# Attention's outputs stay in SBUF with their norms taken there; the first local layer's Q and K operands load during attention

## The chip, the cores and the metric

The kernel runs on one NeuronCore of a Trainium2 chip. The metric is the device time of one execution in microseconds (us), taken over several runs; lower is better. One execution is also recorded by the hardware profiler. Engines are called as the profile calls them: PE (TensorE), DVE (VectorE), ACT (ScalarE), POOL (GpSimd) and SP (SyncE, which here only issues DMAs).

## The reference

The input x is 2048 tokens of 128 features. First comes a global attention with 16 heads of 8 features over all 2048 tokens, with a bias made of relations between tokens; then six local layers, each an attention over windows of 32 tokens (16 heads of 64) and a gated feed-forward.

```
def _layernorm(x, axis=-1, eps=1e-05):
    ...
    return (x - m) / jnp.sqrt(v + eps)

x = L0_attn_hidden_states
x = x + attn(_layernorm(x), ...)        # global attention
x = x + ffn(_layernorm(x), ...)         # six local layers, see below

def ffn(x, ...):
    for i in range(DEPTH):              # DEPTH = 6
        x = attn_layer(shift_tokens(x), Wqkv[i], q_scale[i], k_scale[i], Wo[i]) + x
        x = ffn_layer(shift_tokens(x), ln_g[i], ln_b[i], W1[i], b1[i], W2[i], b2[i]) + x
    return x
```

What matters here is the line between the two: the local layers start from the layer norm of the attention's output x1 = x + attn(...), and x1 itself is added once more at the very end.

## The kernel before, in words

All work goes in blocks of P = 128 tokens, NB = 16 of them. Each engine has its own instruction stream, written out without loops at run time, and the streams meet in semaphores. A `nc.Block()` is a section that all engines enter and leave together.

**Global attention.** The function `attention` is one such section. A block of queries has two units (eight heads each), a unit has 16 steps (one for each block of keys), so there are 512 steps. In each step PE makes two score tiles of 128x1024, called a and b: each from the products `queries_keys` (L529) and the bias `relations` (L537). The a tile runs 24 steps ahead and serves only to find the maximum: DVE takes it into `colmax` (`a_max`, L824, or L820 for the first key block of a unit). The b tile goes through Exp on ACT (L660), and PE multiplies it with the values (`values`, L571). The tiles rotate through three PSUM slots. PE's b products of one step go into the slot of the a tile of the step before, so they wait until DVE has read that one. Beside this, DVE, POOL and ACT make the relation probabilities of blocks to come (`largest`, `recip` L837, `scaled` L758 and others), and SP moves them out to DRAM and back (`quarter_out` L989, `quarter_in` L1002), waiting for POOL each time; SP also loads the next queries (L979).

At fixed steps a unit has small events which PE puts through one PSUM bank, `psM`, and which DVE reads in `read_m`. For every second unit these are, among others, "heads" at step 4 and "proj" at step 6; "max0" (four transposes of `colmax`, L586) comes at step 8. DVE reads "proj" in step 7 (L897): it adds the residual `x_res` and writes `x1_sb`, which SP stores to the DRAM tensor `x1` (`store`, L1031). DVE waits for the former store before it writes `x1_sb` again. After the last block SP waits until all of `x1` has landed (L392 in the profile's waits), and the section ends.

**Between attention and the local layers** there is a second section (L1167 to L1203). SP loads all of `x1` back into `xm`, then the rotary tables `rope` (2 MB), `mask32` and `ident` (L1172), then the 22 loads of the first layer's weights (`load`, L1164). POOL fills six tiles with constants (L1179). DVE waits for the four first loads, takes mean and variance of the 16 blocks (L1192, L1196), POOL raises the variances to the power -0.5 (L1184, L1186), and DVE writes the normed `xa` in two instructions over all blocks (L1200, L1203).

**Local layers.** The third section is a software pipeline of 96 units (six layers of 16 blocks), one step for each unit, with seven steps between a unit's first and last operation. In a step PE transposes the block's input (L1341), ACT copies it shifted by one token to `xsT` (L1433 to L1436), PE projects Q, K and V (L1232), DVE rotates Q and K (L1522 to L1524) with tables that POOL makes (`tab`, L1470), POOL adds and scales, SP copies V's windows (L1664), and so on. PE and POOL wait for all 22 loads of a layer (`w_dma`) before its first unit.

## Time and profile before

| | |
|---|---|
| median of 3 runs | 3207.76 us (3205.29 to 3214.18) |
| the profiled execution, its own time | 3208.75 us |
| its span in the profile | 3206.9 us |
| PE busy | 2957.1 us (92%) |
| DVE busy | 2435.7 us (76%) |
| ACT busy | 2083.1 us (65%) |
| POOL busy | 1978.7 us (62%) |

The span runs from the first to the last instruction that the profile shows; the time has 1.85 us more. A share of busy time is a mean over very different stages, so the stages have to be read one by one: preparation and attention up to 1460.7 us, the section between, and the local layers from 1487.5 us to the end. In the timeline's rows the columns are start, duration, engine, line, operation, output and inputs with their sizes, count, and in square brackets the idle time of the engine before it with what ended it. PEclk is the clock that the chip granted to PE, as a share of 2.4 GHz.

### The profile page before, as it was taken

How to read it: one execution, taken by the hardware profiler on the slowest of the kernel's cores; microseconds unless marked ns; L12 is line 12 of the kernel's file. 1: busy time of each engine (PE TensorE's matmuls, PEld its weight loads, DVE VectorE, ACT ScalarE, POOL GpSimd, SP SyncE). 2: the span in 40 equal slices, each digit the busy share in tenths (PEclk: the TensorE clock that was granted, in tenths of full speed). 3: DMA queues.
4: the chain of work that ended last, by engine and by line, in shares of the span. 5: the costliest groups of instructions: out<-in, count | busy, mean ns of one | idle time of the engine just before them, and what ended most of it. 6: DMA issues, size and time to landing. Idle time of an engine off the chain costs nothing. (4 is left out here: it accounts for less than half of the span.)

```text
span 3206.9 us, 122755 instructions
## 1 busy us (share of the span) xinstructions
PE 2957.1 (92%) x53271; PEld 2271.7 (71%) x53271; DVE 2435.7 (76%) x3493; ACT 2083.1 (65%) x2874; POOL 1978.7 (62%) x1720
## 2 busy tenths in 40 slices
PE   4389999999999999994899999999999999999997
PEld 3267777777777777772677777777777777777776
DVE  4777777777787777743788888887887888888884
ACT  2345555555555555543777877877778787787785
POOL 1635555545554554404777777877777777787783
PEclk8599999999999999997999999999999999999998
DMA  4544454445445444403322233223223322422221
GB/s 119 102 80 85 79 87 83 85 79 86 85 86 86 86 85 85 85 5 107 93 67 71 60 91 82 62 71 96 68 69 83 83 62 68 103 61 72 73 71 43
DMA packets 253992, 251.90 MB, mean 79 GB/s; under 512 B 81999, under 2 KB 198624, under 8 KB 253328
## 3 DMA queue, kind: packets, MB, share of 16 engines
q1 hardware_dynamic: 251776, 243.67, 36.3%
q8 instruction: 421, 6.90, 1.0%
q14 instruction: 115, 0.94, 0.1%
q10 hardware_dynamic: 1680, 0.40, 0.1%
HBM read 96.22 MB, written 40.37 MB: 43 GB/s over the span
## 5 line engine op out<-in xcount | busy, mean ns | idle before, releaser
L660 ACT ACTIVATE prob<-psS 128x1024 f32<-128x1024 f32 x512 | 524.1, 1024 | 588.2 <-PE psS L537 580.6
L824 DVE TENSOR_TENSOR colmax<-psS,colmax 128x1024 f32<-128x1024 f32 x480 | 587.2, 1223 | 298.7 <-PE psS L537 297.5
L537 PE MATMUL psS<-diag,pst 128*128 128x64 bf16 x16384 | 584.6, 194 | 21.7 <-issue 21.7
L537 PEld LDWEIGHTS psS<-diag,pst 128*128 128x128 f16 x16384 | 518.1, 99 | 81.9 <-issue 28.2
L1232 PE MATMUL R<-wqkv,xsT 128*128 128x512 f32 x1152 | 551.9, 602 | 20.2 <-DVE gT L1627 8.7
L529 PE MATMUL psS<-qst,kst 48*128 48x128 bf16 (+1 forms) x8192 | 380.7, 220 | 121.5 <-DMA pst<-p_parts 86.0
L758 POOL TENSOR_TENSOR rel<-rel,rec 128x1024 f32<-128x1024 f32 x64 | 151.8, 2372 | 484.1 <-DVE rec L837 484.1
L529 PEld LDWEIGHTS psS<-qst,kst 48*128 48x128 bf16 (+1 forms) x8192 | 235.3, 95 | 277.6 <-issue 166.9
L1358 ACT ACTIVATE kT<-R 64x1024 f32<-64x1024 f32 x192 | 195.5, 1018 | 255.7 <-PE R L1239 254.6
L1454 POOL TENSOR_TENSOR pr<-pr,mx 128x1024 f32<-128x1024 f32 x96 | 182.6, 1902 | 258.3 <-DVE mx L1539 258.3
L571 PE MATMUL psO<-prob,v 128*9 128x128 f32 x8192 | 326.2, 275 | 11.0 <-issue 9.8
L1232 PEld LDWEIGHTS R<-wqkv,xsT 128*128 128x128 f32 x1152 | 198.0, 192 | 167.3 <-issue 151.9
L837 DVE RECIPROCAL rec<-tot 128x128 f32<-128x128 f32 x256 | 238.7, 939 | 0.0
L1463 POOL TENSOR_TENSOR q<-q 128x1024 f32<-128x1024 f32 x96 | 227.3, 2368 | 9.9 <-DVE q L1524 9.9
L1475 POOL TENSOR_TENSOR k<-k 128x1024 f32<-128x1024 f32 x96 | 227.9, 2374 | 0.0
L1283 PEld LDWEIGHTS psA<-wo,otT 128*128 128x128 f32 x1536 | 186.4, 192 | 44.0 <-issue 44.0
L571 PEld LDWEIGHTS psO<-prob,v 128*9 128x9 f32 x8192 | 173.9, 90 | 42.2 <-issue 13.8
L1252 PE MATMUL R<-kT,qT 128*32 128x128 f32 x6144 | 188.5, 275 | 2.2 <-ACT qT L1346 2.2
L1448 POOL TENSOR_TENSOR kn<-k,rn 128x1024 f32<-128x1024 f32 x96 | 182.6, 1902 | 12.7
L1331 PE MATMUL R<-v,prT 128*32 128x128 f32 x6144 | 187.6, 274 | 2.8 <-ACT prT L1346 2.8
L1458 POOL TENSOR_TENSOR pr<-pr,rn 128x1024 f32<-128x1024 f32 x96 | 182.7, 1903 | 7.5
L1283 PE MATMUL psA<-wo,otT 128*128 128x128 f32 x1536 | 187.0, 275 | 0.0
(191 smaller groups left out, 5896.2 us busy)
## 6 DMA issues: line engine op xcount, KB each, us to landing
v<-vs SPq DMA_DIRECT2D x576, 128.0 KB, 2.4
pst<-p_parts SPq DMA_DIRECT2D x512, 128.0 KB, 4.9
p_parts<-stage SPq DMA_DIRECT2D x64, 512.0 KB, 3.0
v<-vs SPq DMA_DIRECT2D x384, 64.0 KB, 2.1
wqkv<-in_L_ffn_Wqkv SPq DMA_DIRECT2D x18, 512.0 KB
q_stack<-qpart SPq DMA_DIRECT2D x6, 512.0 KB
qst<-q_stack SPq DMA_DIRECT2D x32, 96.0 KB, 5.5
wo<-in_L_ffn_Wo SPq DMA_DIRECT2D x6, 512.0 KB
```

What stands on the lines that cost most here:

```text
L529: pe.matmul(dst[:, hp, P * p:P * (p + 1)], kst[r, pair, P * jb:P * (jb + 1)], qst[r, par, pair, :], start=(p == 0), stop=False, skip_group ...
L537: last = pe.matmul(o, pst[:, par, g, P * jb:P * (jb + 1)], diag[:, par, g, h0:h0 + HH // 2, :], start=False, stop=(g == NG - 1), skip_grou ...
L571: last = pe.matmul(psO[32 * c:32 * c + HD + 1, P * s:P * (s + 1)], v9[:, jb, HH * half + hl, :], prob[:, jb % 2, col:col + P], start=(jb = ...
L660: act.activation(prob[:, st % 2, :], psS[:, slot_of("b", st)].rearrange("p a b -> p (a b)"), ACT.Exp)\
L824: dve.tensor_tensor(dst, src, dst, ALU.max).then_inc(a_read, 1)
L837: dve.reciprocal(rec[:, r, cols], tot[:, r, cols]).then_inc(rr_done, 1)
L1232: last = pe.matmul(R[slot[kind, n]][:, c, :], xsT[:, n % 3, :], w[:, INNER * which + 512 * c:INNER * which + 512 * (c + 1)], start=True, s ...
L1252: last = pe.matmul(o[WIN * w:WIN * (w + 1), P * i:P * (i + 1)], qT[:, par, i, WIN * w:WIN * (w + 1)], kT[:, par, i, :, WIN * w:WIN * (w + 2)],
L1283: last = pe.matmul(psA[:, 0:D], otT[:, i, :], wo[:, n // NB % 2, D * i:D * (i + 1)], start=(i == 0), stop=(i == PAIRS - 1))
L1358: act.activation(kT[r, par, :, hp, WIN:WIN + P], keys[r], ACT.Copy)
L1463: pool.tensor_tensor(q1[:, n % 2, :], q1[:, n % 2, :], q2[:], ALU.add).then_inc(m["q_added"], 1)
L1475: pool.tensor_tensor(k1[:], k1[:], k2[:], ALU.add).then_inc(m["k_added"], 1)
```

## The change

1. Attention adds the projection to `x_res` in place; `x_res` now is the part of `xm` from which the local layers read. SP stores each block to DRAM straight from there, since it is still needed at the end. The wait for the former store goes.
2. For blocks 0 to 14 DVE takes mean and variance right behind that addition (`bn_stats`, `bn_aggr`), and POOL makes the root in `root(blk)`, in windows 1 and 5 of each round of attention.
3. Before the last round of attention SP issues nine loads (`local_first`): the first layer's Q and K weights (512 KB each), the rotary tables of blocks 0 and 1, and six rows of scales.
4. The middle section is gone. The former wait for `x1` to land moves to the first use on DVE (unit 0's L1557) and on SP.
5. In the local section each engine starts with its share: SP issues the other 14 loads of layer 0 (V's weights first), ACT issues `mask32` and the other 14 blocks of `rope`, DVE zeroes `xsT`, `zeros`, `xm`'s first row and `kT`, POOL zeroes a half of `vs` and `v2` behind the first `tab`.
6. `xa` is written block by block (`normed`, one `tensor_scalar`): blocks 0 and 1 at the start, block s + 2 at the start of DVE's step s. Block 15 gets its mean, variance and root there too.
7. Waits for weights are split (`weights_here`): for layer 0 there is one for the early loads, one for V, and one for the rest.

```
@@ attention, DVE, "proj"
-                    if not (isinstance(blk, int) and blk == 0):
-                        dve.wait_ge(x1_dma, blk * 16)
-                    dve.tensor_tensor(x1[:], psM[:, 0:D], xr, ALU.add).then_inc(m_read, 1)
+                    dve.tensor_tensor(x_res[:, blk, :], psM[:, 0:D], x_res[:, blk, :], ALU.add).then_inc(m_read, 1)
+                    if blk < NB - 1:
+                        dve.wait_ge(m_read, n + 1)
+                        if blk > 0:
+                            dve.wait_ge(ln_done, blk)
+                        dve.bn_stats(bn1[:], x_res[:, blk, :]).then_inc(ln_st, 1)
+                        dve.wait_ge(ln_st, blk + 1)
+                        dve.bn_aggr(mv16[:, blk, :], bn1[:]).then_inc(ln_done, 1)
@@ attention, POOL
+            def root(blk):
+                pool.wait_ge(ln_done, blk + 1)
+                pool.tensor_scalar(mv16[:, blk, 1:2], mv16[:, blk, 1:2], 1e-5, None, ALU.add).then_inc(ln_root, 1)
+                pool.wait_ge(ln_root, 2 * blk + 2)
+                pool.tensor_tensor(rs16[:, blk:blk + 1], mv16[:, blk, 1:2], minus_half[:], ALU.pow).then_inc(ln_root, 1)
...
+                    if k % 4 == 1 and not (first and k == 1):
+                        root(it * 2 + k // 4 - 1)
@@ attention, SP
+            def local_first():
+                sp.dma_start(shared["wq0"][:], io["Wqkv"][0, :, 0:INNER]).then_inc(shared["first_dma"], 16)
+                sp.dma_start(shared["wk0"][:], io["Wqkv"][0, :, INNER:2 * INNER]).then_inc(shared["first_dma"], 16)
+                sp.dma_start(shared["rope01"][:], io["rope"][:, 0:2, :]).then_inc(shared["first_dma"], 16)
+                ... six rows of scales ...
...
-                sp.dma_start(dst, x1[:]).then_inc(x1_dma, 16)
+                sp.dma_start(dst[:, blk, :], x_res[:, blk, :]).then_inc(x1_dma, 16)
...
             for it in range(1, 7):
                 body(it)
+            local_first()
             body(7, last=True)
             store(NB - 1, 20 * 7 + 20 - 3 + 3)
-            sp.wait_ge(x1_dma, 16 * NB)
@@ local_layers: the section with L1167 to L1203 is removed whole
@@ local_layers, PE
-                        if n % NB == 0:
-                            pe.wait_ge(m["w_dma"], (n // NB + 1) * (16 * NWL))
+                        weights_here(pe, n, 0)
...
+                        else:
+                            pe.wait_ge(m["xa_ready"], n + 1)
@@ local_layers, ACT
+                act.dma_start(mask32[:], io["mask"]).then_inc(m["mask_dma"], 16)
+                act.dma_start(rope[:], io["rope"][:, 2:NB, :]).then_inc(rope_dma, 16)
                 for s in STEPS:
@@ local_layers, POOL, behind the first tab
+                        if n == 0:
+                            pool.memset(vs[:, 1, :], 0.0).then_inc(m["zero_v"], 1)
+                            pool.memset(v2[:], 0.0).then_inc(m["zero_v"], 1)
@@ local_layers, DVE
+                def normed(b):
+                    dve.tensor_scalar(xa[:, b, :], xm[:, b + 1, :], mv16[:, b, 0:1], rs16[:, b:b + 1], ALU.subtract, ALU.mult)\
+                       .then_inc(m["xa_ready"], 1)
+                dve.memset(xsT[:], 0.0).then_inc(m["zero_kT"], 1)
+                dve.memset(zeros[:], 0.0).then_inc(m["zero_kT"], 1)
+                normed(0)
+                normed(1)
+                dve.memset(xm[:, 0, :], 0.0)
+                dve.memset(kT[:], 0.0).then_inc(m["zero_kT"], 1)
                 for s in STEPS:
+                    n = s + 2
+                    if s >= 0 and n < NB:
+                        if n == NB - 1:
+                            dve.wait_ge(m["ln15"], 5)
+                        normed(n)
...
+                        if n == 0:
+                            dve.wait_ge(x1_dma, 16 * NB)
@@ local_layers, SP
             def _(sp):
+                load(sp, 0)
...
+                        if n == 0:
+                            sp.wait_ge(m["zero_v"], 2)
```

## Rows read from the trace of the kernel before

**Rows 1.** Windows: duration, then busy us (instructions) of each engine, PEclk, DMA, GB/s

```profile
1640.00:3190.00 1550.00, 1527.55 (x18454) 1176.79 (x18453) 1248.21 (x1950) 1215.27 (x1852) 1190.55 (x1243) 1.00 0.30 73
```

**Rows 2.** Timeline from attention's last output to the first unit of the local layers

```profile
1460.40 0.29 DVE L897 TENSOR_TENSOR x_sb<-psM,x_res 128x128 f32<-128x128 f32 x1 [0.58 <-PE psM L597]
1460.79 0.34 SPq L1031 DMA_DIRECT2D x<-x_sb  x1
1462.78 0.11 POOL L1179 MEMSET half<- 128x16 f32 x1 [112.44 <-POOLq L392]
...
1463.67 2.03 SPq L1172 DMA_DIRECT2D rope<-in_rope  x1
1464.57 6.92 POOL L1179 MEMSET v<- 128x8192 f32 x1
...
1474.79 3.19 DVE L1192 BATCH_NORM_STATS2 bn<-xm 128x6 f32<-128x128 f32 x16 [14.10 <-DMA ident<-in_ident]
...
1484.93 2.29 DVE L1203 TENSOR_TENSOR xa<-xa,rs 128x2048 f32<-128x2048 f32 x1
...
1487.53 0.45 PE L1341 MATMUL psA<-ident,xa 128*128 128x128 f32 x1 [27.16 <-PEq L1167]
1488.01 0.27 ACT L1433 ACTIVATE xsT<-psA 64x128 f32<-64x128 f32 x1 [31.14 <-PE psA L1341]
...
1488.68 6.93 PE L1232 MATMUL R<-wqkv,xsT 128*128 128x512 f32 x12 [0.70 <-ACT xsT L1436]
...
1492.22 1.22 DVE L1522 TENSOR_TENSOR q<-R,tab 128x1024 f32<-128x1024 f32 x1 [4.99 <-PE R L1232]
...
1494.72 2.36 POOL L1463 TENSOR_TENSOR q<-q 128x1024 f32<-128x1024 f32 x1 [6.48 <-DVE q L1524]
```

**Rows 3.** Groups by line and shape: count, busy us, mean ns, idle before

```profile
L207 DVE MEMSET v<- 128x256 f32 x1 | 0.3, 272 | 0.2 <-issue 0.2
L1604 DVE TENSOR_SCALAR xn<-xs_f,mv,rstd 128x128 f32<-128x128 f32 x96 | 32.4, 338 | 2.0 <-POOL rstd L1487 2.0
L1588 DVE BATCH_NORM_STATS2 bn<-xs_f 128x6 f32<-128x128 f32 x96 | 27.4, 285 | 23.5 <-DMA xs_f<-xm 23.5
L1592 DVE BATCH_NORM_AGGREGATE mv<-bn 128x2 f32<-128x6 f32 x96 | 17.5, 182 | 3.3
L1487 POOL TENSOR_TENSOR rstd<-var,half 128x1 f32<-128x1 f32 x96 | 54.9, 572 | 8.0
```

**Rows 4.** Timeline of attention around one block's L897, DVE and PE

```profile
771.01 0.28 DVE L897 TENSOR_TENSOR x_sb<-psM,x_res 128x128 f32<-128x128 f32 x1
771.21 0.94 DVE L837 RECIPROCAL rec<-tot 128x128 f32<-128x128 f32 x1
...
772.16 1.23 DVE L820 COPY colmax<-psS 128x1024 f32<-128x1024 f32 x1
...
773.66 0.62 PE L529 MATMUL psS<-qst,kst 48*128 48x128 bf16 x16
...
774.89 1.23 DVE L824 TENSOR_TENSOR colmax<-psS,colmax 128x1024 f32<-128x1024 f32 x1 [0.65 <-PE psS L537]
```

**Rows 5.** Timeline of attention: two places where PE stood still

```profile
661.03 0.40 PE L529 MATMUL psS<-qst,kst 51*128 51x128 bf16 x8 [0.44 <-DVE colmax L824]
661.36 1.11 PE L537 MATMUL psS<-diag,pst 128*128 128x64 bf16 x32
...
692.33 0.34 PE L529 MATMUL psS<-qst,kst 51*128 51x128 bf16 x5 [1.54 <-issue]
692.60 1.54 PE L537 MATMUL psS<-diag,pst 128*128 128x64 bf16 x32
```

**Rows 6.** Timeline of SP where attention's last round begins

```profile
1320.82 1.20 SPq L979 DMA_DIRECT2D qst<-q_stack  x2
1331.32 0.38 SPq L989 DMA_DIRECT2D p_parts<-stage  x1
...
1340.61 0.35 SPq L1031 DMA_DIRECT2D x<-x_sb  x1
```

More of the change, by code:

```diff
@@ L386, with attention @@
 WEIGHTS = 9
-def attention(nc, io, keep):
+def attention(nc, io, keep, shared):
     with ExitStack() as ctx:
@@ L431, in attention @@
         guard_dma = sem("guard_dma")
[L432 removed]
+        ln_st = sem("ln_st")
+        ln_done = sem("ln_done")
+        ln_root = sem("ln_root")
         own_done = sem("own_done")
@@ L1054, in global_attention, with local_layers @@
     prepare(nc, io, keep)
-    attention(nc, io, keep)
-def local_layers(nc, io):
+    attention(nc, io, keep, shared)
+def local_layers(nc, io, shared):
     with ExitStack() as ctx:
@@ L1164, in load @@
                     sp.dma_start(dst, src).then_inc(m["w_dma"], 16)
-        with nc.Block() as block:
-            @block.sync
-            def _(sp):
-                for dst, src in ((xm[:, 1:NB + 1, :], io["x1"].rearrange("(b p) d -> p b d", p=P)),
-                                 (rope[:], io["rope"]), (mask32[:], io["mask"]), (ident[:], io["ident"])):
-                    sp.dma_start(dst, src).then_inc(m["init_dma"], 16)
-                load(sp, 0)
-            @block.gpsimd
-            def _(pool):
-                n = 0
-                for tile, value in ((half1[:], -0.5), (vs[:], 0.0), (v2[:], 0.0), (kT[:], 0.0), (zeros[:], 0.0), (xsT[:], 0.0)):
-                    pool.memset(tile, value).then_inc(m["init_pool"], 1)
-                    n += 1
-                pool.wait_ge(m["init_dve"], 2)
-                pool.wait_ge(m["init_pool"], n)
-                pool.tensor_scalar(mv16[:, :, 1], mv16[:, :, 1], 1e-5, None, ALU.add).then_inc(m["init_pool"], 1)
-                pool.wait_ge(m["init_pool"], n + 1)
-                pool.tensor_tensor(rs16[:], mv16[:, :, 1], half1[:, 0:NB], ALU.pow).then_inc(m["init_pool"], 1)
-            @block.vector
-            def _(dve):
-                dve.wait_ge(m["init_dma"], 16 * 4)
-                for b in range(NB):
-                    last = dve.bn_stats(bn16[:, b, :], xm[:, b + 1, :])
-                last.then_inc(m["init_dve"], 1)
-                dve.wait_ge(m["init_dve"], 1)
-                for b in range(NB):
-                    last = dve.bn_aggr(mv16[:, b, :], bn16[:, b, :])
-                last.then_inc(m["init_dve"], 1)
-                dve.memset(xm[:, 0, :], 0.0)
-                dve.wait_ge(m["init_pool"], 8)
-                dve.tensor_tensor(xa[:], xm[:, 1:NB + 1, :], mv16[:, :, 0:1].broadcast_to([P, NB, D]),
-                                  ALU.subtract).then_inc(m["init_dve"], 1)
-                dve.wait_ge(m["init_dve"], 3)
-                dve.tensor_tensor(xa[:], xa[:], rs16[:].unsqueeze(2).broadcast_to([P, NB, D]), ALU.mult)
@@ L1208, in local_layers, with weights_here @@
+        def weights_here(eng, n, part):
+            l = n // NB
+            if n % NB == 0:
+                if l:
+                    eng.wait_ge(m["w_dma"], l * (16 * NWL))
+                elif part == 2:
+                    eng.wait_ge(v0_dma, 16)
+                elif part == 3:
+                    eng.wait_ge(w0_dma, 16 * (NWL - 9))
+                else:
+                    eng.wait_ge(first_dma, 16 * 9)
         RING = (("S", 2), ("Q", 0), ("kT", 1), ("K", 0), ("V", 0), ("qT", 1), ("pT", 2), ("oT", 3), ("h", 5), ("O", 2))
@@ L1440, in _ @@
             def _(pool):
+                pool.memset(half1[:], -0.5).then_inc(m["ln15"], 1)
                 for s in STEPS:
```

119 lines of the change are left out of this document (78 added, 41 removed).

## The prediction

> **What bounds the kernel now.** I read the windows by stage first, to see where PE is the limit. In the local layers it is: PE is busy for 1527.55 of 1550 us at full clock, against 1248.21 us on DVE and 1190.55 us on POOL [rows 1]. So work taken off DVE or POOL there brings nothing, and work put on them costs nothing as long as PE isn't kept waiting. Attention also runs at PE's pace, but its margin is small: DVE stands only fractions of a microsecond between its instructions [rows 4].
>
> Then I read the timeline over the seam, since the change is mostly there. Attention's last output starts on DVE at 1460.40 us, and the first projection of the local layers starts at 1488.68 us [rows 2]. What fills these 28.28 us can be followed in the rows: the store of the last block (1460.79), its landing and the common exit (first instruction of the next section at 1462.78), the four loads until 1474.79, the norms, the end of the section, a transpose at 1487.53, ACT's copies from 1488.01. It is one chain with nothing beside it on PE, so it lies on the path whole. That is the most that the change can take away here.
>
> Last I read the timeline of one block's projection step in attention, because the change puts new DVE work there, 15 times, and the timeline of SP where the new loads go.
>
> **The seam afterwards.** The section of its own is gone, the round trip of x1 through DRAM too. What is left, step by step:
>
> The exit. SP's last act in attention is to issue the store, 1460.79 + 0.34 = 1461.13. Before, the store had to land first, and the next section began 1.65 later, at 1462.78. Where nothing had to land, at the other section's end, the step was short: DVE's last instruction ended at 1484.93 + 2.29 = 1487.22 and PE began at 1487.53, 0.31 later [rows 2]. I take 1461.13 + 0.37 = 1461.5 for the entry into the local section (bounds 1461.2 and, if nothing of the landing is saved, 1462.8).
>
> DVE's share: `xsT` (384 columns), `zeros`, `normed(0)`. The memset of 256 columns took 0.272 us [rows 3], near 1 ns a column, so `xsT` takes about 0.4; `zeros` 0.1 to 0.2; `normed` is the form of L1604, 0.338 [rows 3]. The first `xa` is ready at 1461.5 + 0.9 = 1462.4, and PE's transpose, 0.48 from its start to ACT's [rows 2], ends near 1463.0.
>
> ACT's share: it issues two DMAs before it may copy. The nearest rows are SP's: 2.03 for all 16 blocks of `rope` [rows 2], so 14/16 x 2.03 = 1.78, and 0.34 for a 64 KB store such as `mask32`. ACT comes free at 1461.5 + 2.1 = 1463.6, and with small gaps at 1463.8. That is later than the transpose, so ACT's issuing ends last at the entry. If an issue on ACT takes twice as long as on SP it is 1465.9.
>
> From ACT's first copy to the projection 1488.68 - 1488.01 = 0.67 [rows 2]. The first projection then starts at 1463.8 + 0.67 = 1464.5 (bounds 1463.7 and 1466.6), in place of 1488.68. **The seam gives 24.2 us**, between 22.1 and 25.0.
>
> What could be late next is checked in turn. The Q weights, the K weights, the scales and the first tables came during attention. DVE must have zeroed `kT` before it rotates Q: 5120 columns at near 0.85 ns (POOL's memset of 8192 took 6.92 us [rows 2]; DVE's own rate by its 256 columns is at most 1.06 ns) are 4.4 to 5.4 us, begun at about 1462.9 behind `normed(1)` and the small memset: free at 1467.3 to 1468.3. The rotation needs the projection, which came 1492.22 - 1488.68 = 3.54 us after its start [rows 2], so at 1468.0. The two meet, at most 0.3 is lost; and if PE still ran at full clock after its short rest, DVE would keep it from gaining more than some 0.7. POOL: 0.11 for `half`, some 0.6 for the first table (a quarter of the 2.36 of L1463's 1024 columns), 0.87 for half of `vs` and 6.92 for `v2` [rows 2], 8.5 in all, so it ends at 1470.0; its first addition came 2.50 behind the start of the rotation [rows 2], so it is wanted at 1470.5. Hidden, by half a microsecond. V's weights are the first of SP's loads, beside 1.8 MB of `rope`. The old four loads, 3.1 MB, were there 1474.79 - 1462.78 = 12.0 us after their section's start [rows 2]; 2.4 MB at that pace are 9.3 us, so 1470.8 at worst. V's projection stands third, some 5 us behind Q's, at 1469.6, and ACT takes its result only 5 us later still. Hidden.
>
> The Trainium skill, "Trainium Kernel Development and Optimization", Key Constraints, says of such splits that DMAs issued from SP, ACT and POOL run on the same 16 DMA engines, and that several issuers save issue time alone. That speaks against moving `rope` to ACT's queue, since it would compete with V's weights; no row of before has two such queues at once. By the rule the sum stays as it is, because the bound above lets both share one rate.
>
> **Attention with the norms in it.** Behind L897 DVE now has `bn_stats` (0.285) and `bn_aggr` (0.182) [rows 3], each behind a wait for the one before, which ends the overlap: today the reciprocal starts 0.20 behind the addition [rows 4], afterwards about 0.31 + 0.31 + 0.09 = 0.71 behind. DVE is 0.51 late in 15 blocks. Who waits: the maximum of the next step (L820) would start at 772.67 and end at 773.90 in the block shown. PE's a products of the following step start at 773.66 [rows 4], because the four transposes of "max0" stand before them in this very step; its b products, which need that maximum read, follow 0.28 later at 773.94. So the margin is 0.04 us less the semaphore: PE waits 0.02 to 0.1. The next maximum has 0.65 of idle time before it [rows 4], so the lateness ends there. I take 0.03 a block, 0.5 us in all. Without the transposes' cover it would be the whole 0.51, so 15 x 0.51 = 7.7 us; that is the upper bound. Below zero it can't go: the store's wait that is removed never showed as idle time before L897.
>
> POOL's root is the pair that L1487 belongs to, 0.572 [rows 3] plus a quarter for the addition, some 0.9 us a block. What hides it is POOL's idle time: it is busy for 62% of the span, and in attention its next work in line, `scaled`, waits for DVE's last reciprocal of the window, which comes steps later. Nothing, then; were POOL the limit, it would be 13 us. The place of `root` comes after DVE's `bn_aggr` in time, so nothing queues behind its wait.
>
> SP issues nine more DMAs before the queries at 1320.82 [rows 6]. At 0.34 [rows 2] to 0.60 each (the two at 1320.82 took 1.20) they take 3 to 5.5 us. SP's next appointment is at 1331.32, and the queries are wanted when the a tiles enter the last block, one step behind the projection stored at 1340.61 [rows 6]. Free up to some 10 us; above that it would cost the excess. Their 1.4 MB run where the DMA queues were mostly empty. I take 0.
>
> **The local layers.** `normed` adds 0.338 x 14 = 4.7 us to DVE, and `xa` in bulk (two instructions) has gone from the seam. PE is the limit from the sixth step on, so at most the steps before that can feel it; there DVE mostly stands before its first instruction of a step. I take 0.3, with 0 and 2 as bounds.
>
> **Sum.** 3208.75 (span 3206.9 and the 1.85 around it) - 24.2 + 0.5 + 0.3 = 3185.35 for an execution like the one profiled. Its time lay 1 us above the median of the runs, so by the median 3207.76 - 23.4 = 3184.4. I predict 3185.
>
> **Rivals.**
> The norms stall PE (rival A). DVE's margin of 0.04 is nothing, and two self-waits more than I count would use it up. For it: PE stood 0.44 us where DVE was late by a similar chain [rows 5]. Against: there no transposes lay between. At the bound, 7.7 us come back: 3192.
>
> The entry is slower than I count (rival B): ACT's issues take twice SP's, the landing of the store counts after all, or the first instructions of the section come late; 2 to 5 us come back, 3187 to 3190. For it: no row shows ACT issuing a large load.
>
> It ends slower (rival C): PE's clock. After a stand of 1.54 us PE's next group took 1.54 us where the same group takes 1.11 behind a stand of 0.44 [rows 5], so a stand of that length costs its own time, 0.43 in this group and, as an estimate from it, up to twice that again in the two groups that follow. If the norm's waits kept PE for 1.5 us in each of 15 blocks, this would be 15 x (1.5 + 1.3) = 42 us: 3226. It decides from 24 / 15 = 1.6 us a block, stand and clock together. Against it: my count is a fiftieth of that, and DVE's own part in full is 0.51.
>
> It hardly moves (rival D): DVE's `tensor_scalar` shuts POOL out. The Trainium skill, "SBUF — State Buffer", Who interferes with whom, says that such an instruction in a two-port mode holds the port that POOL reads through. As a mechanism here: POOL would be held 14 times 0.338, 4.7 us, and the memset of `v2` delayed beside it by 1; even together with A that leaves about 10 us of gain, 3198. The row speaks against the mode: 0.338 for 128 columns is no faster than an addition.
>
> **Chances.** My case 0.72, A 0.10, B 0.08, D 0.02, C 0.04, and 0.04 that several of them together eat all but 9 us. This kernel's runs tell about 0.3% (9.6 us) from no change. Faster takes my case, A, B and D, 0.92; same is the 0.04 of the sum of several; slower is C. The range goes from 3180 (the seam at its best, the clock kept) to 3192 (A in full).
>
> **What the profile will show.** The first L1232-like matmul 4 us behind the last output, not 28; ACT's DMA issues last before its first copy; an idle of under 0.1 on PE before the b products one step after the projection; the same distance from transpose to transpose in the local layers. I am wrong if attention ends more than 2 us later than 1460.7, if DVE's memset of `kT` or V's weights end a wait of PE, or if local steps grow.

## The result and the profile after

| | before | after |
|---|---|---|
| median | 3207.76 us | 3226.15 us (3221.13 to 3227.9, 5 runs) |
| ratio | | 1.0045, 95% interval 1.0031 to 1.0060 |
| span of the profiled execution | 3206.9 us | 3224.8 us |
| attention's first and last output | 281.4, 1460.4 us | 283.3, 1487.7 us |
| first projection of the local layers | 1488.68 us | 1498.69 us |
| unit 0's and unit 6's transposes | 1487.53, 1582.39 us | 1497.51, 1595.05 us |

The changed kernel is slower, by 18 us by the medians and by 10 to 19 us by the interval of the ratio, where 23 us of gain were predicted. The window over the local layers, which answers to [rows 1] (duration, busy us of PE, PE's weight loads, DVE, ACT and POOL, then PEclk, DMA share, GB/s):

```profile
1640.00:3190.00 1550.00, 1528.58 (x18502) 1176.04 (x18501) 1253.50 (x1955) 1215.86 (x1855) 1199.93 (x1251) 1.00 0.29 74
```

PE is as busy there as before (1527.55 us in [rows 1]). So most of the loss is elsewhere. The timeline over the seam, which answers to [rows 2]:

```profile
1487.69 0.29 DVE L907 TENSOR_TENSOR xm<-psM,xm 128x128 f32<-128x128 f32 x1 [0.89 <-PE psM L601]
...
1488.83 0.35 ACTq L1350 DMA_DIRECT2D mask<-in_mask  x1
1488.90 0.73 POOL L1480 TENSOR_TENSOR tab<-rope,scale_rows 128x256 f32<-128x256 f32 x1
...
1489.22 0.45 ACTq L1351 DMA_DIRECT2D rope<-in_rope  x1
1489.28 8.18 DVE L1550 TENSOR_SCALAR xa<-xm,mv,rs 128x128 f32<-128x128 f32 x1
...
1489.56 0.95 POOL L1484 MEMSET vs<- 128x1024 f32 x1
...
1490.45 6.93 POOL L1485 MEMSET v<- 128x8192 f32 x1
...
1497.51 0.47 PE L1343 MATMUL psA<-ident,xa 128*128 128x128 f32 x1 [9.86 <-DVE xa L1550]
...
1498.68 4.33 DVE L1558 MEMSET kT<- 128x5120 f32 x1 [1.01 <-issue]
...
1498.69 3.78 PE L1230 MATMUL R<-wq,xsT 128*128 128x512 f32 x4 [0.70 <-ACT xsT L1444]
```

Two things are to be seen. The last output starts 27.3 us later than in [rows 2], at 1487.69 instead of 1460.40. And the first projection stands 11.00 us behind it, not 28.28 as before and not the predicted 4.1: `normed(0)`, an instruction of a third of a microsecond, lasts 8.18 us on DVE and ends just when POOL's three instructions beside it end (1490.45 + 6.93 = 1497.38).

The span's +17.9 us is then made up like this: attention +27.3, the seam -17.3 (28.28 to 11.00), the steps from unit 0 to unit 6 +2.7 (94.86 to 97.54), the later steps +4.2 (below), and about 1 at the end.

Of the +27.3, 1.9 us lie ahead of the first output, and the first output comes at 276 to 285 us in the kernels below, with no order that an edit would explain. The other 25.4 are in attention between its first and its last output, and not in the work that the change put there. In the waits of PE between the first and the last output (what, who ended it: us in total, times, longest), before and after:

```profile
PE psS L537 <- issue: 21.2, 23, 1.6
PE psS L529 <- DVE colmax L824: 14.5, 36, 0.4
PE psO L571 <- issue: 8.7, 12, 1.4
PE psS L529 <- issue: 8.1, 9, 1.5
```

```profile
PE psS L541 <- issue: 32.7, 27, 2.6
PE psS L533 <- DVE colmax L838: 14.1, 35, 0.4
PE psO L575 <- issue: 11.7, 11, 1.9
PE psS L533 <- issue: 11.5, 9, 1.8
```

The waits for DVE's `colmax` are the same, 14.5 and 14.1 us: PE doesn't wait for the norms. What grew is "issue", time in which PE waits for nothing that the profile shows: 38.0 us before (21.2 + 8.7 + 8.1), 57.2 after (the three rows and 1.3 in a fourth). The windows between first and last output show the rest of it:

```profile
281.40:1460.40 1179.00, 1121.73 (x30012) 867.99 (x30006) 870.04 (x1092) 655.50 (x734) 541.75 (x287) 1.00 0.45 78
```

```profile
283.30:1487.70 1204.40, 1128.37 (x30012) 873.32 (x30006) 876.12 (x1123) 655.99 (x734) 553.56 (x317) 0.99 0.46 77
```

The stretch is 25.4 us longer. 19.2 of it are these stands ("issue stands" from here on), and 6.6 are the same 30012 matmuls taking longer (1121.73 to 1128.37). The stands come every 20 us or so at the same places of PE's instruction stream (37 of the 44 before are at the same matmul after) and are longer there. The same place in before and after:

```profile
837.64 1.02 PE L537 MATMUL psS<-diag,pst 128*128 128x64 bf16 x29 [0.99 <-issue]
```

```profile
852.23 1.73 PE L541 MATMUL psS<-diag,pst 128*128 128x64 bf16 x29 [2.62 <-issue]
```

A stand of 2.62 instead of 0.99 us, and the same 29 matmuls take 1.73 instead of 1.02 behind it. The window of the changed kernel just behind the stand says why, in its last but two column, the granted clock:

```profile
852.00:853.00 1.00, 0.77 (x15) 0.77 (x16) 0.00 (x0) 0.00 (x0) 0.95 (x1) 0.50 0.00 0
```

PE is granted the lower of its two clocks there, 1.2 GHz. Between attention's first and last output that happens 8 times in the changed kernel and 3 times before, each time beside a stand of PE of 1.5 us or more (1.50 to 2.62, and 1.54 to 1.64). The experiments had to find what in the change lengthens the stands.

### The profile page after: what moved, and what is told of

Read it like the earlier page. It is cut to its first block and busy times, and to the rows that moved or that the text cites. A ratio compares the mean times of both kernels' runs of the same rounds, so it can differ in the third digit from the quotient of the medians.

```text
span 3224.8 us, 122812 instructions
## 1 busy us (share of the span) xinstructions
PE 2965.0 (92%) x53271; PEld 2276.7 (71%) x53271; DVE 2452.6 (76%) x3510; ACT 2084.4 (65%) x2874; POOL 1984.3 (62%) x1748
## 5 line engine op out<-in xcount | busy, mean ns | idle before, releaser
L1230 PE MATMUL R<-wq,xsT 128*128 128x512 f32 x384 | 191.5, 622 | 20.3 <-DVE gT L1673 13.2
L1230 PE MATMUL R<-wv,xsT 128*128 128x512 f32 x384 | 181.2, 594 | 4.8 <-ACT sq L1370 4.7
```

Source lines behind the costliest of these rows:

```text
L1230: last = pe.matmul(R[slot[kind, n]][:, c, :], xsT[:, n % 3, :], w[:, 512 * c:512 * (c + 1)], start=True, stop=True)
```

## Experiments

The theories at the start: the norms in attention do it (N); POOL's memset costs the seam its missing 7 us (P); something that isn't work, the tiles' new places in SBUF or the instructions' new places in the stream, does it (layout). Attention is measured below from its first to its last output, "length"; it is read from one profiled execution of each kernel, and the executions of one kernel differ by 10 us and more in time, so lengths that differ by a few us tell little. "Kernel 4" is the kernel of experiment 4. Each time is compared with runs of the kernel before that were made beside it (their medians are 3212.48 us for kernels 1 to 4, and below for the others), so kernels of different groups are best compared by their ratios.

**1. The norms taken out of attention again.** All of `bn_stats`, `bn_aggr` and `root` go from attention to the start of the local section:

```
-                        dve.bn_stats(bn1[:], x_res[:, blk, :]).then_inc(ln_st, 1)
...
-                        dve.bn_aggr(mv16[:, blk, :], bn1[:]).then_inc(ln_done, 1)
...
-                        root(it * 2 + k // 4 - 1)
...
+                for b in range(NB):
+                    last = dve.bn_stats(bn15[:, b, :], xm[:, b + 1, :])
...
+                for b in range(NB):
+                    last = dve.bn_aggr(mv16[:, b, :], bn15[:, b, :])
...
                 normed(0)
```

> The changed kernel with DVE's norms and POOL's roots taken out of attention; all 16 are made at the start of the local section, which costs some 8 us at the seam (3.2 + 1.2 + 0.3 + 2.9 by the old rows). Theory N (the norm instructions lengthen attention, through whatever path): attention's last output comes back from 1487.7 to about 1460 us, the sum of PE's stands that end in 'issue' falls back from 57 to about 36 us, and the kernel takes about 3226 - 27 + 8 = 3207. Theory L (the layout in SBUF, the place of the program or the loads lengthen it, not the norms): attention still ends at 1485 to 1490, and the time is about 3234.

Measured: 3238.64 us, ratio to before 1.0092 (1.0057 to 1.0126). Last output 1486.5, length 1202.4 against the changed kernel's 1204.4; issue stands 58.8 us. The norms do not make attention long. That this kernel is slower than the changed one is the norms' chain, now in front of the first transpose, which comes at 1504.47.

**2. The norms alone, in the kernel before.** DVE takes the same `bn_stats` and `bn_aggr` of `x1_sb`, POOL the root, into tiles that nobody reads; nothing else is changed.

```
                     dve.tensor_tensor(x1[:], psM[:, 0:D], xr, ALU.add).then_inc(m_read, 1)
+                    if blk < NB - 1:
+                        dve.wait_ge(m_read, n + 1)
+                        if blk > 0:
+                            dve.wait_ge(ln_done, blk)
+                        dve.bn_stats(bn1[:], x1[:]).then_inc(ln_st, 1)
+                        dve.wait_ge(ln_st, blk + 1)
+                        dve.bn_aggr(mv1[:, blk, :], bn1[:]).then_inc(ln_done, 1)
```

> The kernel before, with the norms of x1 and their roots made in attention as in the changed kernel, into tiles that nobody reads. Theory N: attention's last output moves from 1460.4 to about 1487, the kernel takes 3230 or more. Theory L: it stays within 3 us of 1460, the kernel within 5 us of 3208.

Measured: 3215.11 us, ratio 1.0014 (0.9999 to 1.0028). Length 1188.1, 9 us more than before's 1179.0, with issue stands as before (39.4). So neither expectation came true: the last output moved to 1469.6, not to 1487 and not within 3 us of 1460. 4.6 us of it are four waits that before doesn't have. One of them, in the timeline of this kernel:

```profile
866.78 1.27 POOL L757 TENSOR_TENSOR tot<-rel 128x512 f32<-128x512 f32 x1 [0.56 <-ACT rel L689]
```

```profile
866.90 1.17 DVE L891 TENSOR_TENSOR gpart<-grest,gpart 128x8 bf16<-128x8 f32 x1
...
868.43 0.27 PE L596 MATMUL psM<-ident,guard 128*24 128x128 f32 x1 [1.16 <-DVE guard L892]
```

A subtraction of 8 columns takes 1.17 us on DVE instead of 0.17, since it falls on an addition of POOL and ends with it, and PE stands 1.16 us. This happens in 4 of 29 blocks, and in none of the kernel before; that DVE's small late steps make the two meet is an inference.

**3. POOL's memsets behind `normed(1)`** in the changed kernel:

```
                         if n == 0:
+                            pool.wait_ge(m["xa_ready"], 2)
                             pool.memset(vs[:, 1, :], 0.0).then_inc(m["zero_v"], 1)
```

> The changed kernel; POOL's two fills at the start of the local section (half of vs, and v2) wait until DVE has written the first two blocks of xa. In the changed kernel the first of these DVE instructions is recorded as 8.18 us and ends with POOL's fill. Theory P (DVE's tensor_scalar is shut out by POOL's fill): each of the two takes 0.1 to 0.4 us, the first projection starts 4 to 5 us behind the last output instead of 11.0, and the kernel is 5 to 7 us faster than the changed one, 3220. Rival: the instruction waits for something else at the entry (its code, a tile); then it still ends 8 us in, and nothing is won.

Measured: 3223.49 us, ratio 1.0039 (1.0015 to 1.0063), 2.7 us under the changed kernel where 5 to 7 were expected, and not clear of noise, since the changed kernel's 1.0045 lies within the interval. DVE and POOL in the timeline:

```profile
1485.35 0.29 DVE L907 TENSOR_TENSOR xm<-psM,xm 128x128 f32<-128x128 f32 x1 [0.89 <-PE psM L601]
...
1486.94 0.42 DVE L1551 TENSOR_SCALAR xa<-xm,mv,rs 128x128 f32<-128x128 f32 x1
...
1487.29 0.33 DVE L1551 TENSOR_SCALAR xa<-xm,mv,rs 128x128 f32<-128x128 f32 x1
...
1488.78 4.33 DVE L1559 MEMSET kT<- 128x5120 f32 x1 [1.02 <-issue]
1493.03 2.54 DVE L1551 TENSOR_SCALAR xa<-xm,mv,rs 128x128 f32<-128x128 f32 x1
...
1495.73 1.20 DVE L1545 TENSOR_TENSOR q<-R,tab 128x1024 f32<-128x1024 f32 x1
```

```profile
1488.57 6.92 POOL L1486 MEMSET v<- 128x8192 f32 x1
```

P is right in its cause: the first two scalings take 0.42 and 0.33 us, and the first projection starts 3.24 us behind the last output (1488.59). But the third one now meets the memset, waits for its end (1495.5) and holds back the rotation of Q to 1495.73. Unit 0 to unit 6 takes 99.18 us in place of 97.54, so 1.6 of the 7.8 us come back there. The steps behind take 4.5 us more than in the changed kernel with no edit in them, which is how far two executions differ. A block moved is not a block removed. DVE's own memset of `kT` takes 4.33 us in both kernels, here beside POOL's memset and in the changed kernel behind it.

**4. Only the places of the tiles.** The kernel before, with `xm`, `ident`, `mv16` and `rs16` in a scope around both parts and an unused tile as large as the changed kernel's early operands. Every attention tile is then where the changed kernel has it, 12,992 bytes higher. No engine executes anything else than before.

```
+        shared = {"xm": sb("xm", [P, NB + 1, D]), "ident": sb("ident", [P, P]), "mv16": sb("mv16", [P, NB, 2]),
+                  "rs16": sb("rs16", [P, NB])}
         with ExitStack() as ctx:
+            ctx.enter_context(nc.sbuf_tensor("room", [P, 2 * INNER + 1024], F32))
             global_attention(nc, ctx, io, shared)
```

> The kernel before with attention's tiles at the addresses of the changed kernel (xm, ident and the small tiles first, 12 KB of room for what the changed kernel loads early), nothing else. If the layout lengthens attention, its last output comes at about 1487 and the kernel takes about 3230; if not, 1460 and 3208.

Measured: 3235.24 us, ratio 1.0071 (1.0047 to 1.0096). Last output 1488.7, length 1208.1, issue stands 59.8. Moving the tiles alone makes all of attention's loss. It is layout, and of the two kinds the place in SBUF, since no instruction has moved.

**5 to 8. Which property of the place?** `pst` is the tile into which SP loads the relation probabilities, 512 landings of 128 KB in attention. It starts 96 bytes past a multiple of 256 in the kernel before and 32 past one in the changed kernel; that is called its offset here. Each of these kernels has one unused tile ahead of attention's tiles:

```
     with ExitStack() as ctx:
+        ctx.enter_context(nc.sbuf_tensor("room", [P, BYTES // 4], F32))
         global_attention(nc, ctx, io)
```

192 bytes (before's place, the changed kernel's offset):

> The kernel before with 192 bytes of unused SBUF per partition ahead of all of attention's tiles, nothing else changed. pst, the first of V's and K's landing tiles, then starts 32 bytes past a multiple of 256 bytes as in the changed kernel (before: 96), while every tile lies within 200 bytes of where the kernel before has it. Theory alignment (the offset within 256 bytes sets how much the landing transfers and PE's instruction fetches disturb each other): attention's last output at about 1488 us in place of 1460, time about 3235 us. Theory position (how far up in SBUF the tiles lie, or which tiles of other stages they share bytes with): last output stays within 3 us of 1460, time 3208 to 3213 us. Theory scatter (every other address gives another value, with no order in it): anything between 1455 and 1495.

12,800 bytes (the changed kernel's place, before's offset):

> The kernel before with 12,800 bytes of unused SBUF per partition ahead of all of attention's tiles (a multiple of 256 and 512, so each tile keeps its offset in 256 and 512 bytes), nothing else changed; the tiles lie within 200 bytes of where the changed kernel has them. Theory alignment: last output stays within 3 us of 1460, time 3208 to 3213 us. Theory position: last output about 1488 us, time about 3235 us. Theory scatter: anything between 1455 and 1495.

160 bytes:

> The kernel before with 160 bytes of room ahead of attention's tiles: pst then starts on a multiple of 512 bytes. Theory alignment: if landing on whole 256-byte pieces is what counts, attention is the shortest here, last output at 1460 or earlier, time at most 3208 us; if it is the offset of another tile (the output stage, 32 bytes past a multiple of 256 here), it can be long, 1488. Theory position: last output within 3 us of 1460, time 3208 to 3213 us. Theory scatter: anything between 1455 and 1495.

The changed kernel with 320 bytes, so that it has before's offset:

> The changed kernel with 320 bytes of room ahead of attention's tiles, so that pst and the tiles around it have the offset within 256 bytes that they have in the kernel before, at the changed kernel's place in SBUF. Theory alignment: attention's last output goes back from 1487.7 to about 1461 us, and the time from 3226 to about 3199 us, faster than before by 9 us. Theory position: last output stays at about 1487, time about 3226 us. Theory scatter: anything between 1455 and 1495, time 3195 to 3233 us.

Measured against 3213.97 us for before: 192 bytes 3234.21 (1.0060, 1.0042 to 1.0078), 12,800 bytes 3212.07 (0.9992, 0.9976 to 1.0008), 160 bytes 3184.61 (0.9911, 0.9878 to 0.9944), the changed kernel with 320 bytes 3207.78 (0.9984, 0.9970 to 0.9998). The position is out: 12,800 bytes higher costs nothing. The offset is in: 192 bytes alone cost as much as the changed kernel's places. (Kernel 5's last output, 1476.8, is not the expected 1488, but the profiled execution was its fastest, 10 us under its median.) And an offset that neither kernel had makes the kernel before 0.9% faster with 160 unused bytes. The changed kernel's last output comes down by 17.6 us to 1470.1, not by the expected 26.7; the rest is looked at with the norms, below.

**9 and 10. Which tile?** The landing tile `pst` moved by 160 bytes with all others kept at their offsets, and the reverse:

```
+        sb("room_a", [P, 40])          # 160 bytes
         pst = sb("pst", [P, 2, NG, S], FP16)
+        sb("room_b", [P, 24])          # 96 bytes
```

> The kernel before with pst alone moved by 160 bytes, onto a multiple of 256; the tiles behind it move by 256, so their offsets within 256 stay, and those ahead of it (qst, kst, v9, coef) stay where they are. The whole move by 160 (b3) had brought the last output from 1460.4 to 1437.1 us and the time to 0.991 of before. Theory pst (the 512 landings of V's and K's parts are what the offset acts on): last output about 1437 to 1442, time about 3185 us. Theory qst (the landing of the queries' rows, 256 bytes each): last output about 1460, time about 3208 to 3213 us. Theory both in part: 1445 to 1455, time 3192 to 3203 us.

> The complement: every tile of attention but pst moved to the offset that it has in b3 (qst on a multiple of 128), pst kept at 96 past a multiple of 256 as before. Theory pst: last output about 1460, time 3208 to 3213 us. Theory qst: about 1437 to 1442, time about 3185 us. Theory both in part: 1445 to 1455, time 3192 to 3203 us.

Measured against 3214.58: `pst` alone 3188.29 (0.9913, 0.9892 to 0.9934), all but `pst` 3213.53 (0.9994, 0.9979 to 1.0008). The gain from 96 to 0 is `pst`'s, wholly.

**11 to 13. What must its offset be a multiple of?** The expectations below count offsets from a multiple of 512, where before is at 352. `pst` alone at 64, 128 and 256 bytes past a multiple of 512.

> The kernel before with pst alone moved, to 64 bytes past a multiple of 512 (before: 352 past one, changed kernel: 32). So far the offset modulo 512 and the last output: 0 gives 1437, 352 gives 1460, 32 gives 1477 to 1489. Theory 64 (a landing whose rows start on a multiple of 64 bytes is written whole): last output about 1437 to 1442, time about 3186 us. Theory 512 or 256 (only whole pieces of that size count): an offset of 64 is as bad as others, last output 1455 to 1490, time 3205 to 3235 us.

> pst alone moved to 128 bytes past a multiple of 512. Theory 64, and a theory 128: last output about 1437 to 1442, time about 3186 us. Theory 256 or 512: 1455 to 1490, time 3205 to 3235 us.

> pst alone moved to 256 bytes past a multiple of 512. Theory 64, 128 or 256: last output about 1437 to 1442, time about 3186 us. Theory 512: 1455 to 1490, time 3205 to 3235 us.

Measured against 3215.26: 3224.68 (1.0023, 1.0008 to 1.0037), 3213.86 (0.9995, 0.9980 to 1.0010) and 3183.76 (0.9905, 0.9884 to 0.9925). So 64 and 128 are not enough and 512 isn't needed: it takes a multiple of 256. All of these together, by the offset of `pst` from a multiple of 256 (share: what the packets of SP's queue, q1, took of the 16 DMA engines between 300 and 1430 us):

```
offset  kernel                 length    issue stands   q1 share
0       before, 160 bytes      1160.8    23.2           39.7%
0       pst alone, +160        1156.7    21.0           40.3%
0       pst alone, at 256      1158.2    21.3           40.0%
96      before                 1179.0    38.0           44.3%
96      before, 12,800 bytes   1180.3    40.4           44.4%
96      all but pst            1183.7    44.2           43.5%
128     pst alone, at 128      1185.8    44.0           43.7%
64      pst alone, at 64       1193.3    48.5           44.6%
32      before, 192 bytes      1197.0    56.4           45.3%
32      places of the change   1208.1    59.8           46.3%
32      the change             1204.4    57.2           46.2%
```

At 32 `pst` was never moved alone; that the rest of the way from 96 to 32 is its doing too is an inference from kernel 10, where moving all the others changed nothing. The transfers are the same. The view of the DMAs from 300 to 1430 us has these lines (packets, MB, share of 16 engines) for before, for the changed kernel and for `pst` at 256:

```profile
q1 hardware_dynamic: 100430, 85.88, 44.3%
```

```profile
q1 hardware_dynamic: 102080, 87.72, 46.2%
```

```profile
q1 hardware_dynamic: 99818, 85.33, 40.0%
```

On a multiple of 256 the transfers occupy the engines for 40% of the time, elsewhere for 44 to 46%, and a landing of 128 KB takes 4.6 us where it takes 4.9 (before) and 5.1 (after). The bytes in the stretch differ by up to 3% from kernel to kernel; per MB the share is 0.47% at `pst` on 256, 0.52 before and 0.53 after. The waits of PE in the same kernel, `pst` at 256:

```profile
PE psS L531 <- DVE colmax L826: 14.5, 36, 0.4
PE psS L539 <- issue: 12.1, 18, 1.6
PE psO L573 <- issue: 5.7, 10, 1.1
PE psS L531 <- issue: 3.5, 5, 1.0
```

21.3 us of stands instead of 38.0; the waits for `colmax` stay. The Trainium skill, "DMA: Bandwidth & Descriptors", How a descriptor splits into AXI transactions, says that a descriptor is cut into transactions that start at multiples of 256 bytes, so that one which doesn't start on such a multiple can need one more; it says so of reads, and here it is the written side. `pst`'s rows are 512 elements of two bytes. As an estimate by that rule, a row makes four transactions on a multiple and five off it. The step between 0 and everything else agrees with it. The order among the rest does not: worked out by the same rule, an offset of 128 should cost most and 32 least, and here 128 is about as good as 96 and 32 is the worst.

**14. The changed kernel with `pst` on a multiple of 256** (480 bytes of room ahead of attention):

> The changed kernel with 480 bytes of room ahead of attention's tiles, which gives each of them the offset within 512 bytes that it has in b3. If the offset is all that ailed the changed kernel's attention: last output about 1438 to 1441 us in place of 1487.7; with its own seam (11.0 us), ramp and layer loads as measured, the span is about 3224.8 - 48 = 3177 us, time 3175 to 3182 us, 0.989 to 0.991 of before. If the changed kernel's place in SBUF or its other instructions in attention count too: last output over 1450, time over 3190 us.

Measured: 3181.30 us (3175.09 to 3193.87), ratio 0.9894 (0.9873 to 0.9916) to before. Last output 1442.8, 2 us later than expected, the time as expected: 45 us under the changed kernel, from 480 unused bytes.

**15. The same, with the seam and the loads mended.** DVE scales four blocks before POOL zeroes, `v2` is zeroed in two halves, and layers 1 to 5 load in before's order:

```
-                        if n == 0:
-                            pool.memset(vs[:, 1, :], 0.0).then_inc(m["zero_v"], 1)
-                            pool.memset(v2[:], 0.0).then_inc(m["zero_v"], 1)
+                        if n < 2:
+                            if n == 0:
+                                pool.wait_ge(m["xa_ready"], 4)
+                                pool.memset(vs[:, 1, :], 0.0).then_inc(m["zero_v"], 1)
+                            pool.memset(v2[:, n], 0.0).then_inc(m["zero_v"], 1)
...
                 normed(1)
+                normed(2)
+                normed(3)
...
-            jobs = ([wqkv_part(0), *scales], [wqkv_part(1), *rest[0:3], *biases[0:3]], [wqkv_part(2), *rest[3:7], *biases[3:6]])
+            jobs = ([wqkv_part(0), *rest[0:2], *biases[0:3], rest[2]],
+                    [wqkv_part(1), *rest[3:6], *biases[3:6], *scales[0:2]],
+                    [wqkv_part(2), rest[6], *scales[2:6]])
```

> c3 with two more edits. First, DVE scales blocks 0 to 3 ahead of POOL's zeroing, which waits for them and is done in two halves, for unit 0 and unit 1 (3.5 us each in place of 6.9 at once). Second, the weights of layers 1 to 5 are loaded in the order of the kernel before. Theory port (DVE's scaling can't start while POOL zeroes): the first projection stands about 4 us behind attention's last output in place of 11.0; of the 7 us saved some 2 to 4 come back where rotation meets the second half; gain over c3 3 to 6 us. Theory order (the changed order of the loads costs 4 us over the five layers): another 3 to 5 us. Together 6 to 10 us under c3, time about 3168 to 3174 us. If both are noise of the profile: same as c3, 3175 to 3182 us.

Measured: 3175.51 us (3171.19 to 3185.6), ratio 0.9878 (0.9856 to 0.9900): the fastest of all, 5.8 us by the medians under kernel 14, though the two intervals overlap, and 1.5 us above the range expected. Its seam in the timeline:

```profile
1446.78 0.29 DVE L907 TENSOR_TENSOR xm<-psM,xm 128x128 f32<-128x128 f32 x1 [0.58 <-PE psM L601]
...
1448.37 0.42 DVE L1554 TENSOR_SCALAR xa<-xm,mv,rs 128x128 f32<-128x128 f32 x1
...
1448.71 0.84 DVE L1554 TENSOR_SCALAR xa<-xm,mv,rs 128x128 f32<-128x128 f32 x3
...
1460.90 3.52 POOL L1489 MEMSET v<- 128x4096 f32 x1
...
1464.37 2.34 POOL L1493 TENSOR_TENSOR k<-k 128x1024 f32<-128x1024 f32 x1
```

Unit 0's transpose comes 2.1 us behind the last output, where kernel 14 has 9.8. But POOL's second half stands in front of its addition for K, which starts at 1464.37, 17.6 us behind the last output; unit 0 to unit 6 takes 100.5 us in place of 96.7. So half of the 7.7 us is given back. The loads bring the rest: see the local layers in the next section.

## Why the prediction was wrong

**The step that failed is one that the prediction didn't write down.** It took attention's end from the kernel before (1460.40), added 0.5 us for the norms, and put the new places of the tiles at nothing by not naming them. That the change also moves `x_res` and the early weights into a scope around attention, and with them every attention tile by 12,992 bytes, is in the diff as a declaration. It brought `pst` from 96 to 32 bytes past a multiple of 256. Kernel 4 shows what that costs, by itself: attention 29 us longer (1208.1 against 1179.0) with no instruction changed. The prediction named the sign that it would be wrong ("attention ends more than 2 us later than 1460.7"), and that is what happened, by 27.

**The seam, -24.2 predicted, -17.3 measured.** The section went, and its 28.28 us with it. The entry was right: SP's store ends at 1488.42, the first instructions of the new section start at 1488.81, 0.39 later (predicted 0.37). ACT's issues took 0.35 and 0.45 us, not 2.1, so they were oversized by 1.3, and PE waits for DVE's `xa` and not for ACT. `xsT` 0.38 (0.4), and the entry without POOL in the way is 3.24 us in kernel 3 (predicted 4.1). The missing 7 us are DVE's `normed(0)`, costed at 0.338 and lasting 8.18. Rival D had the two engines and the instruction, but in the wrong order: it let DVE hold POOL for 0.338 us at a time, and dismissed it with the duration of L1604, a row of another stage. Here POOL was first (its `tab` started at 1488.90, DVE's scaling at 1489.28) and held on through three instructions in a row to 1497.38. The Trainium skill, "SBUF — State Buffer", Who interferes with whom, says of a DVE instruction in a two-port mode and a GpSimd instruction that whoever issues first has the shared ports for the whole instruction and the other is blocked fully. Kernels 3 and 15 agree: the scalings that DVE runs ahead of POOL's memset lose nothing (0.42 and 0.33 us), and the one that meets it half done waits for its end. The price should have been taken from the longest POOL instruction beside it: 6.92 us stood in [rows 2].

**The norms, +0.5 predicted.** On PE's critical waits the step was right: 14.1 us for `colmax` against 14.5. DVE's timeline in the changed kernel shows the predicted form:

```profile
867.33 0.28 DVE L907 TENSOR_TENSOR xm<-psM,xm 128x128 f32<-128x128 f32 x1
867.64 0.29 DVE L912 BATCH_NORM_STATS2 bn<-xm 128x6 f32<-128x128 f32 x1
...
867.97 0.18 DVE L914 BATCH_NORM_AGGREGATE mv<-bn 128x2 f32<-128x6 f32 x1
868.07 0.92 DVE L851 RECIPROCAL rec<-tot 128x128 f32<-128x128 f32 x1
```

0.31 + 0.33 + 0.10 = 0.74 from the addition to the reciprocal, 0.71 predicted. Yet at equal offset attention is longer with the norms than without: at 0, 1165.2 and 1164.6 against 1156.7 to 1160.8; at 96, 1184.8 (kernel 8) and 1188.1 (kernel 2) against 1179.0 to 1183.7. That is 4 to 8 us at 0 and 1 to 9 at 96, where 0.5 was put and 7.7 was the bound. In kernels 2, 14 and 15, 4.6, 3.5 and 1.2 us of it are waits for the `guard` of the kind shown under 2; the rest is not found. At 32 there is no such difference (1202.4 without them in kernel 1, 1204.4 with), and single executions differ by as much, so its size is open.

**The local layers, +0.3 predicted, +6.9 measured.** 2.7 are in the first six steps; 1.6 of these are in the first two (8.95 and 17.52 us against 7.92 and 16.92), where the rotation of Q starts 1.2 us late behind the memset of `kT`, for which the prediction allowed 0.3. The other 4.2 are where a layer's weights arrive: from unit 6 on, what the steps take over 17.215 us each sums to 11.5 us before and to 15.7 after. The change also spread the loads of layers 1 to 5 in another order over SP's three parts, which the prediction did not price. The sums of the kernels with the old order are 9.0 to 13.5 us (before, kernels 2, 4 to 7, 9 to 13, and 15 with 12.9), those with the new order 15.4 to 20.2 (after, 1, 3, 8, 14). They don't overlap; kernel 15 against 14 is the order put back, 12.9 against 18.0. PE's largest wait there is for DVE's `gT`: 13.2 us in 8 times in the changed kernel and in kernel 14, 8.7 in 8 before, 8.2 in 6 in kernel 15. Which of the transfers keeps DVE is open, and kernel 15 alone tests the order.

**Sum.** 3206.9 + 27.3 (places of the tiles, with the norms' share in it) - 17.3 + 6.9 + 1 = 3224.8. The rivals' mechanisms: A fell at the place it named, since PE doesn't wait for `colmax` more than before. B's entry was quicker than counted. C named 3226 for a slower result, and the time was 3226, but that is luck: no stand of PE ends with a norm. Its second half was right: PE is granted 1.2 GHz beside its longest stands, and its matmuls take 6.6 us more in all. What makes the stands long is another matter. V's weights and the memset of `kT` (4.33, predicted 4.4 to 5.4) ended no wait of PE, as predicted. Yet the memset isn't hidden: it starts 1.01 us behind the instruction before it, ends at 1503.01, and DVE's rotation of Q starts at 1503.41, 4.72 us behind the projection's start where it was 3.54.

**What is shown and what is not.** Shown is that `pst`'s offset alone sets 21 to 37 us of attention (1156.7 and 1158.2 at 0, 1179.0 to 1193.3 at 96, 128 and 64; at 32 all tiles were moved together, to 1197.0 to 1208.1), that the same transfers then hold the DMA engines longer, and that PE's stands without a visible cause grow with it.

What these stands are, the traces show by time. They record each packet of the instruction queue, 421 of them (6.90 MB, 16 KB each) in both kernels. 236 lie between attention's first and last output, one for every 127 matmuls and their weight loads, and the issue stands are a whole number of such pieces apart (510, 383 or 638 matmuls and so on). In all 17 traces each issue stand, 744 in all, ends 1.18 to 1.94 us behind the end of such a packet; of all instants in attention only 15% do. By these times PE stands there for its next instructions. And the packets ahead of a stand are those that come in beside landings. For the stand at 837.64 of the kernel before the packet came from 834.31 to 836.36, and the view of the DMAs says of the two microseconds ahead of it (832.3 to 834.3; over 100% where packets overlap):

```profile
q1 hardware_dynamic: 383, 0.26, 118.0%
```

In the same view of 841.1 to 843.1, ahead of the next packet but one, behind which PE doesn't stand, q1 has no packet. As a mean over attention q1's share in these two microseconds is 114% ahead of the packets with a stand in both kernels, and 28 and 24% ahead of the others. No experiment moved these packets by themselves, so that the landings hold them up rests on these times and on the offset's effect. Why an offset of 32 is worse than 64, and 64 than 96 and 128, is open.

## What to carry to other kernels

Before a change is costed by its instructions, look at what it does to addresses: a tile put in front of others moves them all, and for a tile into which DMAs land all the time (here 512 landings of 128 KB in rows of 1 KB) a start on a multiple of 256 bytes is worth a run. Here 160 unused bytes were worth 0.9%, more than the whole edit that was meant to help, and the sign that something is off is a growth of "issue" stands with unchanged waits for other engines.

Where DVE and POOL both start work at a seam, let the short one that others wait for go first and cut the long one in pieces; and follow where the blocked time goes next, as it came back at the third scaling and then at K's addition.

What an edit is worth can be judged only at equal addresses: the change gains 6 us by the medians at offset 96 (kernel 8, 3207.78 against 3213.97, an interval that just leaves out 1), and at offset 0, with what it broke mended, some 9 to 11 us by the ratios (0.9878 against 0.9905 to 0.9913, with intervals that overlap), where as it stood it lost 18.

## What the runs showed of the hardware

- The offset of a landing tile: at 0 from a multiple of 256 bytes, q1's packets take 39.7 to 41.0% of the DMA engines and a landing of 128 KB 4.5 to 4.6 us; at 32 to 128, 43.5 to 46.6% and 4.9 to 5.2 us.
- PE's stands without a visible cause follow it, 21 to 26 us in attention at 0, 38 to 46 at 96 and 128, 48.5 at 64, 56 to 60 at 32. Each ends 1.18 to 1.94 us behind the end of a 16 KB packet of the instruction queue.
- PE's granted clock was 0.5, of 2.4 GHz, at 8 places of the changed kernel's attention, each beside a stand of 1.50 to 2.62 us, at 3 before (1.54 to 1.64 us), and at none in kernels 9 and 13.
- A POOL memset blocks DVE's `tensor_scalar` for its whole length, here over three POOL instructions in a row (8.18 us for 0.34), but not DVE's own memset (4.33 us with and without it).
- A POOL `tensor_tensor` blocked a DVE `tensor_tensor` of 8 columns until its end (1.17 us for 0.17, 4 times in kernel 2).
- A load issued by ACT took ACT 0.35 (mask) and 0.45 us (14 blocks of `rope`), where SP took 2.03 for 16 blocks [rows 2], right behind another load of 1 MB.
